# Transposing the attention probabilities of two heads in four by VectorE squares and a round trip through DRAM

## The reference, cut to what matters

```
q, k, v = x @ wq, x @ wk, x @ wv          # 16 heads of q, 4 of k and v
scores  = scale * q @ k.T, masked above the diagonal
probs   = softmax(scores)
x       = layernorm(x + (probs @ v) @ wo)
```

## Time and profile before

| what | us |
|---|---|
| median of three runs | 1833.12 |
| the profiled execution, its own time | 1836.27 |
| its span in the trace | 1834.5 |
| PE busy | 1774.3 (97%) |
| DVE busy | 1238.0 (67%) |
| ACT busy | 823.1 (45%) |
| POOL busy | 799.0 (44%) |
| mean granted clock of PE, share of full | 0.991 |

### The profile page before, as it was taken

How to read it: one execution, slowest core, us unless ns; L and a number is a source line. 1 busy time by engine, 2 the same in 40 slices (tenths; PEclk the granted TensorE clock), 3 DMA queues, 4 the chain that set the end, 5 groups by cost and what they waited for, 6 DMA issues and landing times.

```text
span 1834.5 us, 33331 instructions
## 1 busy us (share of the span) xinstructions
PE 1774.3 (97%) x9290; PEld 1502.0 (82%) x9290; DVE 1238.0 (67%) x3881; ACT 823.1 (45%) x2058; POOL 799.0 (44%) x1093
## 2 busy tenths in 40 slices
PE   8999999999999999999999999999999999999982
PEld 7888888888888888888888888888888888778872
DVE  5566467776777577757775777677776777763355
ACT  4444344434444444544454444454444443434454
POOL 6775345544554333323332333233323334666564
PEclk9999999999999999999999999999999999999996
DMA  9665443335333455454444445454445338545788
GB/s 329 223 226 195 164 141 116 116 110 168 116 116 110 150 162 153 150 174 149 154 150 159 134 152 160 154 177 158 150 133 198 135 107 314 173 161 166 251 314 318
DMA packets 156287, 315.83 MB, mean 172 GB/s; under 512 B 23008, under 2 KB 66176, under 8 KB 145600
## 3 DMA queue, kind: packets, MB, share of 16 engines
q1 hardware_dynamic: 137808, 273.74, 44.2%
q0 software_dynamic: 18288, 39.80, 7.1%
HBM read 226.25 MB, written 87.23 MB: 171 GB/s over the span
## 4 chain that ended last, share of the span: by engine, by line
PE 85%; DVE 4%; issue 3%; POOL 2%; DMA 2%; ACT 1%; DVEq 0%; POOLq 0%; ACTq 0%; SPq 0%
PE psum L1541 23%; PE psum L1543 23%; PE psum L1542 23%; PE psum L1568 7%; PE psum L2298 2%; PE psum L2299 2%; PE psum L2300 2%; PE psum L372 1%; DMA token_rows<-x,ids_now 1%; ACT probs L1818 1%; PE psum L788 1%; DVE pT_lo L1942 1%; POOL expert_weights L1435 1%; POOL probs L1415 0%; DMA chosen_rows<-y_rows,slot_now 0%
## 5 line engine op out<-in xcount | busy, mean ns | idle before, releaser
L1415 POOL TENSOR_SCALAR probs<-probs,row_inv 128x128 f32<-128x128 f32 (+3 forms) x512 | 308.0, 625 | 435.1 <-DVE row_inv L1939 433.2
L1818 ACT ACTIVATE probs<-probs,neg_max 128x512 f32<-128x512 f32 (+3 forms) x512 | 282.4, 554 | 361.4 <-DVE neg_max L1931 359.4
L1541 PE MATMUL psum<-xT_hi,w_hi 128*128 128x512 f32 x640 | 252.5, 394 | 0.7 <-DVE qT_lo L1956 0.7
L1931 DVE CUSTOM_DVE_ANT_0 probs<-psum,causal 128x512 f32<-128x512 f32 (+3 forms) x512 | 223.4, 487 | 42.7 <-issue 20.4
L1543 PE MATMUL psum<-xT_hi,w_lo 128*128 128x512 f32 x640 | 250.2, 391 | 0.0
L1542 PE MATMUL psum<-xT_lo,w_hi 128*128 128x512 f32 x640 | 249.9, 390 | 0.0
L1942 DVE TENSOR_TENSOR pT_lo<-psum,pT_hi 128x512 fp32r<-128x512 f32 (+1 forms) x384 | 206.5, 593 | 19.7 <-ACT pT_hi L1828 19.5
L1828 ACT CAST pT_hi<-psum 128x512 fp32r<-128x512 f32 (+1 forms) x384 | 172.3, 526 | 65.2 <-PE psum L1568 65.2
L1541 PE MATMUL psum<-wo_hi,oT_hi 128*128 128x512 f32 x496 | 196.8, 397 | 0.0
L1543 PE MATMUL psum<-wo_hi,oT_lo 128*128 128x512 f32 x496 | 194.0, 391 | 0.0
L1542 PE MATMUL psum<-wo_lo,oT_hi 128*128 128x512 f32 x496 | 193.6, 390 | 0.0
(11 more groups left out here) (250 smaller groups left out, 3870.4 us busy)
## 6 DMA issues: line engine op xcount, KB each, us to landing
w_hi<-split_qk_weights SPq DMA_DIRECT2D x140, 256.0 KB, 2.7
w_lo<-split_qk_weights SPq DMA_DIRECT2D x140, 256.0 KB, 3.0
wo_hi<-split_out_weights SPq DMA_DIRECT2D x27, 1024.0 KB, 5.5
wo_lo<-split_out_weights SPq DMA_DIRECT2D x27, 1024.0 KB, 7.6
expert_weights_hi_lo<-split_expert_weights SPq DMA_DIRECT2D x8, 2048.0 KB, 10.0
x_in<-in_L_attn_x_dram SPq DMA_DIRECT2D x8, 1024.0 KB, 7.3
expert_weights<-fill SPq DMA_DIRECT2D x16, 512.0 KB, 4.4
piece_raw<-expert_weights SPq DMA_DIRECT2D x16, 512.0 KB, 5.9
```

What stands on the lines that cost most here:

```text
L1415: last = pool.tensor_scalar(p, p, row_inv[:, buf, i:i + 1], 1.0, ALU.mult, ALU.mult)
L1541: pe.matmul(dst, hi_s, hi_m, start=start, stop=False)
L1818: last = act.activation(probs[:, buf, a:a + w], probs[:, buf, a:a + w], ACT.Exp, bias=neg_max[:, buf, i:i + 1], scale=-1.0, accum_out=row_ ...
L1931: last = dve.tensor_tensor_reduce(probs[:, buf, a:a + w], psum[:, BANK_S + bank, col:col + w], causal[:, T - w:T], -1.0, -MASKED, ALU.add, ...
```

## The change

From sequence 1 on, in all iterations but the last (`is_moved`, 27 of the 32), the heads n and n+2 are no longer turned by PE. DVE turns the 32x32 squares inside `probs` (`turn_blocks`, five instructions for the ten blocks) into a new tile `blocks`; SP writes it to a DRAM tensor (`move`, 640 KB), waits for that, and reads it back with four DMAs of 32 partitions each, which put every square in its place (`moved`). ACT then makes the high part in one instruction and DVE the low part in one (`moved_pT`), both from SBUF. PE still turns the heads n+1 and n+3.

The order is rewritten around it. On PE, query(n+2) comes before the first filler, scores(n+2) before the second; a "group" iteration forms its key and uses its banks as a "first" one does (`banks_as`); the transposes of n+3 stand between the two queries. On DVE, ACT, POOL and SP the steps follow suit. To make room, the buffers for the pieces of the expert weights (`piece_raw`, `piece_hi`, `piece_lo`) go from two to one.

```diff
@@ helpers
+def is_moved(kind, route):
+    return route and kind != "end"
+def is_key_first(kind, route):
+    return kind == "first" or is_moved(kind, route) and kind == "group"
+def banks_as(kind, route):
+    return "first" if is_key_first(kind, route) else kind
@@ sync: SP
+        def move(it, k, free):
+            wait_apart(sp, s_blocks, moved_number(it, k) + 1, s_passed)
+            sp.dma_start(strips[k], F.blocks[:].rearrange("p j f -> p (j f)")).then_inc(s_moved, 16)
+            wait_apart(sp, s_pt_lo, free, s_passed)
+            wait_apart(sp, s_moved, 32 + MOVES * moved_number(it, k), s_passed)
+            for j in range(SIDE):
+                src = strips[k, :, j * PACK // SIDE:(j + 1) * PACK // SIDE].rearrange("(i p) f -> p i f", p=SQUARE)
+                sp.dma_start(F.moved[j * SQUARE:(j + 1) * SQUARE], src).then_inc(s_moved, 16)
+
         def iteration(b, g, it, kind, route, job):
+            if is_moved(kind, route):
+                move(it, 0, 3 * n)
             if route and kind == "first":
                 wait_apart(sp, s_r_out, 16 * b, s_passed)
                 route_load(sp, R, it - TT, ...)
...
             slot(4, it + 1, after)
+            if is_moved(kind, route):
+                move(it, 1, 3 * (n + 2) + 3)
@@ tensor: PE
             scores(n + 1, 1)
+            if moved:
+                pe.wait_ge(s_q_lo, n + 2)
+                query(2, it, BANK_A)
...
             filler(0 if kind == "first" else 1)
-            pe.wait_ge(s_q_lo, n + 2)
-            query(2, it, BANK_A)
+            if moved:
+                scores(n + 2, 0)
+            else:
+                pe.wait_ge(s_q_lo, n + 2)
+                query(2, it, BANK_A)
...
-            transposes(n, 0)
+            if not moved:
+                transposes(n, 0, kind, route)
...
                 filler(1 if kind == "first" else 2)
-            transposes(n + 1, 1)
-            scores(n + 2, 0)
+            transposes(n, 1, kind, route)
+            if not moved:
+                scores(n + 2, 0)
...
             query(3, it, BANK_A)
+            if kind == "first" and moved:
+                filler(2)
+                scores(n + 3, 1)
...
             filler(3)
             if kind == "batch":
-                turn_x(b + 1, (2, 3))
-            scores(n + 3, 1)
+                turn_x(b + 1, (0, 1) if moved else (2, 3), route)
+            if not (kind == "first" and moved):
+                scores(n + 3, 1)
+            if kind == "batch" and moved:
+                turn_x(b + 1, (2, 3), route)
...
-            query(0, it + 1, bank_of_query(0, kind))
+            query(0, it + 1, bank_of_query(0, banks))
+            if moved:
+                transposes(n, 3, kind, route)
@@ scalar: ACT
+        def moved_pT(n, it, k):
+            act.wait_ge(s_moved, 16 + MOVES * (moved_number(it, k) + 1))
+            act.wait_ge(s_o, n + 2 * k)
+            act.copy(pT_hi[:, 0].rearrange("p (b i c) -> p b i c", i=SIDE, c=SQUARE),
+                     F.moved[:].rearrange("p i (b c) -> p b i c", c=SQUARE)).then_inc(s_pt_hi, 3)
...
             exps(n + 1, 1)
+            if moved:
+                qT(n + 2, 0, BANK_A)
@@ vector: DVE
+        def turn_blocks(n, it, k):
+            dve.wait_ge(s_norm, n + 2 * k + 1)
+            dve.wait_ge(s_moved, 16 + MOVES * moved_number(it, k))
+            blocks = F.blocks[:].rearrange("p j (b c) -> p b j c", c=SQUARE)
+            for i in range(TT):
+                keys = range(min(i + 1, TT - 1))
+                at = [KEY_AT[j] // P + i - j for j in keys]
+                src = probs[:, 0, ROW_AT[i]:ROW_AT[i] + len(keys) * P].rearrange("p (b j c) -> p b j c", j=SIDE, c=SQUARE)
+                last = dve.transpose(blocks[:, at[0]:at[-1] + 1:3], src)
...
             maxima(n + 1, 1)
+            if moved:
+                qT(n + 2, 0, BANK_A)
+                turn_blocks(n, it, 0)
+                inverse(n + 1, 1)
...
                 route_variance(dve, R, tt)
             if kind != "first":
                 add_rows(it - 1, 1, "group")
-            inverse(n + 1, 1)
+            if moved:
+                dve.wait_ge(s_blocks, moved_number(it, 0) + 1)
+                maxima(n + 2, 0)
+            else:
+                inverse(n + 1, 1)
+                qT(n + 2, 0, BANK_A)
+                pT(n, 0, moved)
...
             if kind != "end":
                 qT(n + 3, 1, BANK_A)
+            if moved:
+                turn_blocks(n, it, 1)
+            if early and moved:
+                route_logits(dve, R, tt, (2,), products)
+            if moved:
+                moved_pT(n, 0)
```

More of the change, by code:

```diff
@@ L1457, in iteration @@
             n = it * G
-            if route and kind != "first":
+            if route and kind == "end":
                 route_rstd(pool, R, it - TT)
             normalize(n + 1, 1)
+            if route and kind not in ("first", "end"):
+                route_rstd(pool, R, it - TT)
             if job == "scatter":
@@ L1734, in iteration @@
                 return
-            if kind == "first":
+            if kind == "first" and not moved:
                 filler(2)
@@ L1748, in iteration @@
             values_first()
-            if kind in ("group", "batch"):
+            if not key_first:
                 pe.wait_ge(s_q_lo, n + 4)
@@ L1763, in iteration @@
                 pe.wait_ge(s_k_lo, it + 2)
-            query(1, it + 1, bank_of_query(1, kind))
-            transposes(n + 3, 1)
+            query(1, it + 1, bank_of_query(1, banks))
+            if not moved:
+                transposes(n, 3, kind, route)
             scores(n + 4, 0)
             values_second()
-            out_rows(0, it, kind, route)
+            out_rows(0, it, banks, route)
             if kind == "batch":
@@ L1878, in iteration @@
                 qT(n + 3, 1, BANK_A)
-            pT(n + 1, 1)
-            exps(n + 2, 0)
-            if kind == "first":
+            pT(it, 1, kind, route)
+            if not moved:
+                exps(n + 2, 0)
+            if kind == "first" and not moved:
                 v(b, 2)
@@ L2037, in iteration @@
                 route_normalize(dve, R, tt)
-            inverse(n + 2, 0)
-            if early:
+            if not moved:
+                inverse(n + 2, 0)
+            if early and not moved:
                 route_logits(dve, R, tt, (2, 3), products)
@@ L2046, in iteration @@
                 qT(n + 3, 1, BANK_A)
+            if moved:
+                turn_blocks(n, it, 1)
+            if early and moved:
+                route_logits(dve, R, tt, (2,), products)
+            if moved:
+                moved_pT(n, 0)
             if late:
                 route_logits(dve, R, tt, (1, 2), products)
-            if kind == "batch":
+            if kind == "batch" and not moved:
                 low_xT(dve, F, psum, b + 1, (0, 1), BANKS_PT[:2])
@@ L2053, in iteration @@
             if kind == "batch":
+                low_xT(dve, F, psum, b + 1, (0, 1) if moved else (2, 3), BANKS_PT[:2])
+            maxima(n + 3, 1)
+            if early and moved:
+                route_logits(dve, R, tt, (3,), products)
+            if kind == "batch" and moved:
                 low_xT(dve, F, psum, b + 1, (2, 3), BANKS_PT[:2])
-            maxima(n + 3, 1)
             if route:
@@ L2064, in iteration @@
                 count_later(dve, N, upper, q)
-            if kind == "first":
+            if key_first:
                 kT(it + 1)
-            oT(n, 0, 0, kind)
+            oT(n, 0, 0, banks)
             if kind == "end":
-                pT(n + 2, 0)
+                pT(n, 2, moved)
             if route:
@@ L2082, in iteration @@
                 count_later(dve, N, upper, q)
-            if kind in ("group", "batch"):
+            if not key_first and kind != "end":
                 kT(it + 1)
-            if kind != "end":
-                pT(n + 2, 0)
+            if kind != "end" and not moved:
+                pT(n, 2, moved)
             if route:
```

230 lines of the change are left out of this document (141 added, 89 removed).

## The result

| | before | after |
| --- | --- | --- |
| median, us (lowest to highest) | 1833.18 (1832.2 to 1833.85) | 1889.22 (1885.83 to 1894.24) |
| ratio to before, 95% interval | 1 | 1.0308 [1.0284, 1.0333] |
| span of the profiled execution, us | 1834.5 | 1892.5 |
| mean granted clock of PE | 0.991 | 0.981 |

What follows compares the result with a forecast made beforehand. PE, busy 97% of the span, was taken as the bound. 14 x 1.1 (group) + 7 x 1.9 (first) + 6 x 2.6 (batch) = 44.3 us on 1836.27 gave 1880.6, at the median 1877; range 1835 to 1920.

Steps and rivals of the forecast that it cites:

- What goes: PE's transposes: 1.10 us a head, two heads in each of 27 iterations, 59.4 us if nothing comes in their place.
- The first wait: PE at scores(n+2) waits for the low part of query n+2, starting at 898.55 instead of 897.00: 1.55 us.
- The second wait: PE at row 2 waits for row 1 to be added, behind 1.73 us of turning on DVE: 1.64 us.
- Rival C: Slower still: turnings cost 2.75 us each, the second wait grows by 1.0 in each iteration: 1905; chance 0.10.
- A group iteration: Each of the 14 moved "group" iterations becomes 1.1 us longer, the rest beyond the two waits costed at nothing.
- Rival E: The trip is late and the values wait, on top of the rest: 1 us each, 1904; chance 0.06.
- A "first" iteration: Each of seven: scores(n+2) 0.8 late, scores(n+3) 3.3 late behind the routing rows, less 2.2: +1.9 us.
- A "batch" iteration: Each of six: the two waits of a group, plus about 1.2 at turning x and 0.3 at the key: +2.6 us.
- B: Faster: PE stays without gaps and gains all 59.4 us, 1774; with just one wait, 1817; chance 0.13 whole or in part.
- the draw D: Routing rows in time (-23), short turnings (-10), no wait in "batch" iterations (-9) together: 1835; chance 0.05.

Runs made afterwards that it cites:

- e10: e9 plus, in batch iterations, ACT's high part of xT 2 and 3 ahead of the exponentials and DVE's low parts of xT moved earlier; 1804.54 us.
- e1: Changed kernel, with ACT making the high part of query n+2 ahead of the exponentials of n+1 in moved iterations; 1840.51 us.
- e6: e4 without the trip through DRAM, ACT and DVE reading the turned squares where DVE left them (values from misplaced squares); 1815.20 us.
- e3: Changed kernel, with SP issuing the load of the routing rows ahead of the first trip of the squares in "first" iterations; 1866.46 us.
- e4: Changed kernel with three edits: query high part ahead of exponentials, row 1 added ahead of the turnings, routing rows loaded ahead of the first trip; 1820.02 us.
- e9: e4 with PE's wait for oT_lo directly ahead of the transposes of n+3 instead of ahead of query(n+4); 1815.04 us.
- e5: e4 with one router product less ahead of maxima(n+3) on DVE and, in batch iterations, low parts of xT earlier; 1824.02 us.
- e8: e4 with a gap on purpose: DVE forms the low part of query n+2 five times in each moved iteration; 1913.65 us.
- e7: Changed kernel with each turning of squares done twice, into the same place; 2018.59 us.
- e11: e4 with a shorter gap on purpose: DVE forms the low part of query n+2 three times in each moved iteration; 1853.02 us.

## Why the prediction was right

The forecast was slower, 1877 with 1855 to 1900 as its own range; 1889 lies in it. Step by step:

- **What goes**: 1.10 us for one head. Right: PE is busy 42.46 in place of 44.55 in a group iteration, and 42.40 in e10.
- **The first wait**, forecast 1.55, measured 1.50, for the reason given: ACT takes the exponentials of n+1 first. e1 undoes just that and the wait is gone.
- **The second wait**, forecast 1.64 behind 1.73 us of turning; measured 1.37 behind 1.66. The pitch of DVE's other instructions of the same widths was the right price for an instruction that no row showed, also with squares of 32 written at strides. Rival C (2.75) is out by this row. The estimate of 3.11 us from the 311 ns of the Trainium skill (VectorE: DVE Perf Modes, section The three transpose paths) is out too. By the Trainium skill's pace of one element per cycle per lane (Vector Engine (DVE) Microarchitecture Reference, section 3.8) the time would grow with the columns. It does: 128, 256 and 384 columns have means of 302, 403 and 536 ns, 0.8 to 1.0 ns for a column more. No run here shows the length of a cycle.
- **A group iteration**: forecast +1.1, measured +0.7 to +0.95 in the second loop (44.57 to 45.3 and 45.5) and +0.8 in the mean of all 14. The trip costs next to nothing, as forecast: write 3.0 us to landing, reads 3.3, and e6 gains 4.8 in all by leaving it out. Rival E is out.
- **A "first" iteration**: forecast +1.9, measured +2.2 to +4.7, +3.2 in the mean. The mechanism is the one told (e3: -22.8). The waits were not too small: scores(n+3) waited 2.0 to 4.1, 2.9 in the mean of seven, where the forecast had 3.3, and scores(n+2) 0.4 in the mean, where it had 0.8. The load of the rows came 7 us later than before, where the forecast had 10. What the term lacks is the half clock, 1.7 us in each of the seven.
- **A "batch" iteration**: forecast +2.6, measured +2.4 and +2.6 in the first loop, and in the second +3.6, or +5.6 with a stretch of half clock. Of its two waits for xT_lo the forecast had 1.2 and 0.3; they measured 0.75 and 0.65.
- **What the sum left out**: the forecast is 12 us short, and against the profiled spans 58.0 - 44.3 = 13.7. By the periods, group iterations came 14 x 0.27 = 3.8 under it, "first" ones (mean +3.16) 7 x 1.26 = 8.8 over, batch ones (mean +3.89) 6 x 1.29 = 7.7 over: +12.7. All nine half-clock stretches, 18.7 us, lie in "first" and batch iterations. So what the sum lacked is that a gap can cost more than its length: without the clock's part the "first" term would have been high rather than low, and the batch term nearly right.
- **The rivals.** B, the draw D and C were each a statement that one wait would not be there or be larger; the waits were there, at the size told. The draw would have needed the routing rows in time, which e3 shows to be worth 22.8 (forecast in D: 23). That this agrees so well is in part luck: 17.6 of it are the wait, the rest is the clock.

What I had not seen is how little held the 59.4 us back. No helper was full (DVE 69%, ACT 43%, POOL 41%): the three edits of e4 move one step each, e9 a wait, e10 three steps of the batch iterations, and the same turnings and trips then give 1804.5, a gain of 28.5 against before. Of the 59.4 that is a half. The profiled spans say where the rest is: they differ by 31.7, and of the 27.7 to 59.4 PE idles 19.7 (79.9 in place of 60.2) and is busy 8.0 longer than before less the transposes (1722.9 in place of 1714.9). Between 265 and 1400 us its waits are 21.8 us, against 6 in before. A version without these waits was not tried.

## What to carry to other kernels

When an engine that is full is relieved of work, as PE is here, the instructions behind come earlier, and a helper whose order was fitted to the old time can be late though it is far from full: list them by the order they take work in, not by how busy they are, and move the late one's step ahead of what it does not depend on. A wait that is removed uncovers the next in the same iteration, so price an edit by running down to the iteration's end. Read such a wait iteration by iteration and not as a sum over the run: in e5 it fell in one kind of iteration and rose in another. A gap in TensorE can cost more than its length (e8: 1.4 times).

## What the hardware showed that I had not expected

- The granted clock of TensorE fell to half behind gaps of 1.5 to 4 us, in some cases and not in others: between 225 and 1540 us none in the kernel before (it has two outside, at 27 and 1769 us), and in the moved iterations nine in the kernel after (18.7 us), 36 in e7 (74.8), 17 in e8 behind 27 gaps of 2.0 to 4.1 us; in e11 none behind its gaps of 1.0 to 1.7 us at scores(n+2), and three behind other waits of 1.7 to 1.9. The loss of a stretch was 1.64 to 1.72 us in every run, or twice that (3.36 to 3.42).
- VectorE turned ten 128x128 blocks of 32-bit data in squares of 32 in 1.66 us, against 1.10 us of TensorE for moving them through the array. Groups of the kernel after by form (busy us, mean ns):

```profile
L2060 DVE STREAM_TRANSPOSE probs_blocks<-probs 128x384 f32<-128x384 f32 x108 | 53.8, 536 | 0.0
...
L2048 DVE TENSOR_TENSOR pT_lo<-probs_moved,pT_hi 128x1280 fp32r<-128x1280 f32 x54 | 80.2, 1485 | 0.4 <-DVE route_logits L700 0.4
```

- The low part read in runs of 32 columns took 1485 ns for 1280 columns; the one that reads single elements at strides took 2200 for 1024.
- A trip of 640 KB to DRAM and back in four parts (DMA issues of the kernel after: KB each, median us to landing) was cheap beside all other transfers:

```profile
probs_strips<-probs_blocks SPq DMA_DIRECT2D x54, 640.0 KB, 3.0
probs_moved<-probs_strips SPq DMA_DIRECT2D x216, 160.0 KB, 3.3
```
